# The end of an attention stage in an order written out by hand, with its output weights loaded in four pieces

## What is computed

```
x = x + _L0_xattn_ref(_layernorm(x), ctx_1024, cos, sin, ..., Wq, Wkv, Wo, bo)
    # lat, ctx = layer_norm(...); q = lat @ Wq; k, v = split(ctx @ Wkv)   16 heads of 64
    # k = apply_rope(k, cos, sin)
    # attn = clip(q k^T / 8, -11, 11); attn = softmax(attn); out = attn v
    # return out @ Wo + bo                     out: 4 x 128 x 1024, Wo: 1024 x 512
x = x + _L0_attn_ref(_layernorm(x), qkv_w, qkv_b, proj_w, proj_b)
x = x + _L0_ffn_ref(_layernorm(x), router_w, sg, su, sd, wg, wu, wd)
```

## Time and profile before

| | us |
|---|---|
| median of 3 runs | 1446.51 (1441.37 to 1452.56) |
| the profiled execution | 1454.4, its span 1452.7 |
| PE busy | 1394.5 (96%) |
| DVE, ACT, POOL busy | 850.0, 797.3, 833.6 |
| loop of `attend`, a step | about 8.1 |
| step 32 of the last batch to the start of `mix` | 1109.18 to 1164.85 |

### The profile page before, as it was taken

One profiled execution on the slowest core, in us unless ns is written; L12 is line 12 of the kernel. 1 busy time (PEld: TensorE's weight loads), 2 busy tenths in 40 slices (PEclk: granted clock), 3 DMA queues, 4 the chain that ended last, 5 costly groups with the idle time before them and its releaser, 6 DMA issues. The chain is left out here.

```text
span 1452.7 us, 25242 instructions
## 1 busy us (share of the span) xinstructions
PE 1394.5 (96%) x8758; PEld 1139.3 (78%) x8758; DVE 850.0 (59%) x1420; ACT 797.3 (55%) x1237; POOL 833.6 (57%) x723
## 2 busy tenths in 40 slices
PE   5899999999999999999999999999998889999998
PEld 3578888888788888878888888888887566766664
DVE  6456565666466566655565666656554356657564
ACT  3356566665566665656666656656555312346652
POOL 3267677776667776766777777777765324110002
PEclk9999999999999999999999999999999989899999
DMA  7567766766666676656677666776767380369994
GB/s 241 178 118 130 123 118 110 132 116 135 114 120 123 111 130 110 139 100 129 113 131 122 123 130 118 130 123 107 138 107 163 116 326 0 131 219 365 357 370 150
DMA packets 115219, 218.44 MB, mean 150 GB/s; under 512 B 13312, under 2 KB 49152, under 8 KB 108928
## 3 DMA queue, kind: packets, MB, share of 16 engines
q1 hardware_dynamic: 111920, 209.00, 63.8%
q0 software_dynamic: 1280, 4.20, 0.9%
q10 hardware_dynamic: 1872, 3.41, 0.6%
HBM read 132.67 MB, written 16.78 MB: 103 GB/s over the span
## 5 line engine op out<-in xcount | busy, mean ns | idle before, releaser
L605 POOL TENSOR_TENSOR p_parts<-probs,p_parts 128x512 fp32r<-128x512 f32 x256 | 340.3, 1349 | 252.2 <-ACT p_parts L660 252.2
L660 ACT ACTIVATE p_parts<-probs 128x512 fp32r<-128x512 f32 x256 | 147.7, 625 | 245.5 <-PE banks L914 237.9
L768 DVE TENSOR_TENSOR probs<-banks,probs 128x1024 f32<-128x1024 f32 x128 | 156.7, 1224 | 164.1 <-ACT probs L668 164.1
L709 ACT ACTIVATE probs<-probs 128x1024 f32<-128x1024 f32 x128 | 135.9, 1062 | 142.6 <-POOL probs L612 142.5
L866 PE MATMUL banks<-wv_hi,x_hi 128*128 128x512 f32 x512 | 208.5, 407 | 4.9 <-PEq L170 4.9
L867 PE MATMUL banks<-wv_lo,x_hi 128*128 128x512 f32 x512 | 202.8, 396 | 0.0
L881 PE MATMUL banks<-x_hi,wk_hi 128*128 128x512 f32 x512 | 201.8, 394 | 0.0
L868 PE MATMUL banks<-wv_hi,x_lo 128*128 128x512 f32 x512 | 201.8, 394 | 0.0
L883 PE MATMUL banks<-x_hi,wk_lo 128*128 128x512 f32 x512 | 199.6, 390 | 0.0
L882 PE MATMUL banks<-x_lo,wk_hi 128*128 128x512 f32 x512 | 199.3, 389 | 0.0
L910 PE MATMUL banks<-p_parts,v_hi 128*65 128x128 f32 x1024 | 192.0, 224 | 0.6 <-POOL p_parts L605 0.6
(11 more groups left out here) (291 smaller groups left out, 2694.5 us busy)
## 6 DMA issues: line engine op xcount, KB each, us to landing
queries<-q_scratch SPq DMA_DIRECT2D x256, 128.0 KB, 6.0
keys<-wo_room SPq DMA_DIRECT2D x128, 256.0 KB, 5.6
keys<-turned_odd SPq DMA_DIRECT2D x128, 256.0 KB, 5.6
row_room<-in_ctx SPq DMA_DIRECT2D x64, 256.0 KB, 6.2
wo_room<-in_down SPq DMA_DIRECT2D x10, 1024.0 KB, 7.1
wo<-in_gate SPq DMA_DIRECT2D x8, 1024.0 KB, 8.2
gate_raw<-in_up SPq DMA_DIRECT2D x8, 1024.0 KB, 10.2
up_raw<-in_gate SPq DMA_DIRECT2D x7, 1024.0 KB, 8.2
```

The lines of the kernel that those rows point to most:

```text
L605: nc.gpsimd.tensor_tensor(p_parts[:, 1, j, :], probs[:, pair % 2, j, :], p_parts[:, 0, j, :].bitcast(F32), ALU.subtract).then_inc(p_lo_rea ...
L768: nc.vector.tensor_tensor(mine, ps_s[:, :, :, 0, :].rearrange("p j i n -> p (j i) n"), mine, ALU.add).then_inc(s_taken, 1)
```

## The change

The steps that all engines share now end with step 31 of the last batch, and what follows is written out by hand for each engine.

- PE: in step 31 the value product is left out and put behind `weigh(26)`, in two halves around `score(28)`. From there on single output products, one, two or three at a time, stand between the scores and the weighings. A batch's sum now starts with tiles 4 to 7 (the second half of `wo`). All 8 products of batch 2 stand at the very end, behind the last `turn_sums`.
- ACT, DVE, POOL: the same instructions in another order. The low parts of the last two rotated keys move from POOL to DVE (`rope_low`). The four bias additions are parted in two pairs, the splits of the self attention's weights come later.
- `wo` is now two tensors of 4 tiles, `wo_first` and `wo_second`, in the first buffers of `x_hi` and `x_lo`, which are dead once chunk 2 of the last batch is done. SP loads it in four pieces of 512 KB in steps 25 to 28, for which it waits in step 24 for the key product of step 23. The loads of `x`, `bo` and of the three weights follow the last keys at once.
- The split weights of the self attention lie elsewhere (second buffers of `x_hi` and `x_lo`, `wk_hi`, `wk_lo`). The room of `wk_lo` (now `late_room`) is in use until the last qkv product, so in `mix` SP waits for `qkv_done` 12 where it waited for `wo_done`.

```
@@ SP
+                    wait(sp, k_ready, BATCH * BSTEPS - STEPS)
+                i = t - (BSTEPS - STEPS + 1)
+                if 0 <= i < KT:
+                    half, k = i // 2, i % 2 * 2
+                    sp.dma_start(wo[half][:, k:k + 2, :], d["wo"].rearrange("(t p) n -> p t n", p=P)[:, 2 * i:2 * i + 2, :]
+                                 ).then_inc(keep["wo_landed"], 16)
...
             run(sp, step)
+            wait(sp, s_ready, last_step - SCORE_LAG)
+            for pair in range(BSTEPS - 3, BSTEPS):
+                load_queries(LAST, pair)
+            store_keys(LAST, BSTEPS)
+
+            wait(sp, v_ready, last_step)
+            sp.dma_start(keep["x3"][:], d["x"].rearrange("b n d -> n b d")).then_inc(x_landed, 16)
...
@@ DVE
             run(dve, step)
+            rotate(LAST, 31)
+            finish(LAST, 25)
+            combine(LAST, BSTEPS, 0)
+            add_values(LAST, 26)
+            combine(LAST, BSTEPS, 1)
+            rope_low(0)
+            rope_low(1)
+            take_scores(LAST, 28)
+            values_low(LAST, 31)
+            finish(LAST, 26)
+            add_values(LAST, 27)
+            take_scores(LAST, 29)
+            finish(LAST, 27)
+            add_values(LAST, 28)
+            add_bias(0)
+            add_bias(1)
+            take_scores(LAST, 30)
...
@@ PE
+            for k in ks:
+                    if k == KT:
+                        wait(pe, keep["wo_landed"], 16 * KT)
+                        wait(pe, k_turned, last_step)
+                        wait(pe, keep["attn_t_ready"], max(2 * whose + 1, whose + 4 if whose else 0))
...
             run(pe, step)
+            values(LAST, 31, (0, 1))
+            score(LAST, 28)
+            values(LAST, 31, (2, 3))
+            turn_early(0)
+            turn_early(1)
+            turn_sums(LAST, 26)
+            weigh(LAST, 27)
+            score(LAST, 29)
+            turn_early(2)
+            turn_early(3)
+            project_early(0, (4, 5))
+            turn_sums(LAST, 27)
+            weigh(LAST, 28)
+            score(LAST, 30)
+            project_early(0, (6, 7))
+            turn_early(4)
+            project_early(0, (0,))
+            turn_sums(LAST, 28)
+            weigh(LAST, 29)
+            score(LAST, 31)
+            turn_early(5)
+            project_early(0, (1, 2, 3))
+            turn_sums(LAST, 29)
+            project_early(1, (4, 5))
+            weigh(LAST, 30)
+            project_early(1, (6, 7))
+            turn_sums(LAST, 30)
+            project_early(1, (0, 1))
+            weigh(LAST, 31)
+            project_early(1, (2, 3))
+            turn_sums(LAST, 31)
+            project_early(2, (4, 5, 6, 7, 0, 1, 2, 3))
...
@@ mix, SP
-            sp.wait_ge(wo_done, BATCH)
+            sp.wait_ge(qkv_done, 3 * BATCH)
```

More of the change, by code:

```diff
@@ L486, in run @@
                     step(b, t)
-            for t in range(STEPS, BSTEPS + VALUE_LAG + 2):
-                step(BATCH - 1, t)
+            for t in range(STEPS, BSTEPS):
+                step(LAST, t)
         def exists(b, t):
@@ L497, in ends_batch @@
             return exists(b, pair) and pair // STEPS % CHUNKS == CHUNKS - 1
-        def ends(b, t, n):
-            return isinstance(b, int) and b == BATCH - 1 and t == BSTEPS + n
         def row_tile_of(b, t):
@@ L633, in _ @@
             run(pool, step)
+            for pair in range(BSTEPS - VALUE_LAG, BSTEPS):
+                low_probs(LAST, pair)
+                clip(LAST, pair + 1)
         @block.scalar
@@ L696, in step, with exponents @@
+            def exponents(b, pair):
+                if exists(b, pair):
+                    wait(act, clipped, b * BSTEPS + (pair + 1))
+                    nc.scalar.activation(probs[:, pair % 2], probs[:, pair % 2], ACT.Exp, scale=SCALE).then_inc(probs_ready, 1)
+            def step(b, t):
+                high_probs(b, t - VALUE_LAG)
+                copy_scores(b, t - SCORE_LAG)
+                values_high(b, t - 1)
+                rope_high(b, t, 0)
                 tile = row_tile_of(b, t)
@@ L704, in step @@
                     out.then_inc(rows["full_ready"], 1)
[L706 to L712 removed]
+                exponents(b, t - SCORE_LAG)
+                rope_high(b, t, 1)
                 tile = row_tile_of(b, t - 1)
@@ L801, in split_low, with rope_low, add_bias @@
                                         ALU.subtract).then_inc(keep["qkv_lo_ready"], 1)
+            def rope_low(n):
+                group = BATCH * GROUPS - 1
+                slot = group % 2
+                part = parts_of(slot)[n]
+                wait(dve, rope_hi, 2 * group + (n + 1))
+                wait(dve, rope_lo, 2 * group + n)
+                nc.vector.tensor_tensor(part.bitcast(F32R), part, highs_of(slot)[n].bitcast(F32), ALU.subtract).then_inc(rope_lo, 1)
+            def add_bias(i):
+                if i == 0:
+                    wait(dve, x_landed, 32)
+                nc.vector.tensor_tensor(keep["x3"][:, i, :], keep["x3"][:, i, :], bo[:], ALU.add).then_inc(keep["x_ready"], 1)
             def step(b, t):
+                last = isinstance(b, int) and BSTEPS * b + t == last_step - 1
                 rotate(b, t - 1)
                 add_values(b, t - VALUE_LAG - 1)
-                if ends(b, t, 4):
-                    split_low(1)
                 combine(b, t, 0)
@@ L812, in step @@
                 take_scores(b, t - SCORE_LAG)
-                if ends(b, t, 3):
-                    split_low(0)
                 combine(b, t, 1)
                 values_low(b, t - 1)
-                finish(b, t - VALUE_LAG - 1)
+                if not last:
+                    finish(b, t - VALUE_LAG - 1)
                 tile = row_tile_of(b, t + 2) if t >= 1 else None
@@ L823, in step @@
                     row_tile_variance(nc, rows, dve, whole, tile % ROW_TILES)
-                if ends(b, t, 1):
-                    wait(dve, x_landed, 32)
-                    for i in range(BATCH):
-                        nc.vector.tensor_tensor(keep["x3"][:, i, :], keep["x3"][:, i, :], bo[:], ALU.add).then_inc(keep["x_ready"], 1)
                 if t % BSTEPS == STEPS - 1 and t > STEPS:
@@ L1828, in program @@
         keep = {"ident": sb("ident", [P, P]), "minus_half": sb("minus_half", [P, 8])}
-        keep["x_hi"] = sb("x_hi", [P, 2, KT, CHUNK], F32R)
+        with nc.sbuf_tensor("x_hi", [P, 2, KT, CHUNK], F32R) as keep["x_hi"]:
+            pass
+        keep["wo"] = [sb("wo_first", [P, 2, KT, DIM])[:, 0]]
         room = sb("row_room", [P, BATCH - 1, INNER])
```

174 lines of the change are left out of this document (89 added, 85 removed).

## The result

| | before | changed |
|---|---|---|
| median of 7 runs | 1446.76 us (1441.37 to 1452.56) | 1435.82 us (1432.80 to 1439.64) |
| ratio to before | | 0.9921, 95% interval 0.9895 to 0.9947 |
| the profiled execution | 1454.4, span 1452.7 | 1435.8, span 1434.1 |
| first score of step 31 to the start of `mix` | 63.79 | 48.89 |
| start of `mix` to the first qkv product | 14.57 | 11.02 |

The change gains 10.9 us, 0.8%. The two profiled executions lie 18.6 us apart, and the whole of it, 14.90 + 3.55 = 18.45 us, is in the two stretches that the change touches.

The account below looks back on a forecast made before the run. PE bounds the kernel, losing tail time to idleness and half clock. Tail -16.3, dip +1.2, `bo` and keys +0.6, `mix` start -3.3 gave -17.8 us; -17.5 from the 1446.5 median gave 1429 us, range 1422 to 1439.

Parts of the forecast that it names:

- PE's work: Tail from the point matching 1109.18: scores, transposes, sums with weighings and products at full clock, together 36.0 us.
- `bo`: Tail: bias lands at 1122.1, additions precede `take_scores(30)`, slack nearly nothing; 0.6 us taken for this and late keys.
- The first hole: Tail, second transpose group: PE waits 2.2 us for DVE's low part of step 31's value tile to free PSUM.
- The later holes: Tail: PE waits 0.5 us at `turn_sums(28)` for the scores of pair 30, then 0.2 us at the next.
- a dip behind the first hole: Tail: half clock after the 2.2 us wait at the second transpose group costs 0 to 1.5 us; 1.2 taken.
- The rival in which the whole tail runs at half clock: From the second transpose group PE's 35 us of work take twice as long; 1449 us, chance 0.03.
- The start of `mix`: First transposes to first qkv product: PE keeps full clock, DVE limits; 11.2 us for 14.6, so -3.3 us.
- The block's end: End of the tail: 0.35 us from the last instruction to the next block, as before.
- The pieces of `wo`: Steps 25 to 28: early loads behind key stores cost nothing; uncovered, each 1 MB pair up to 4.6 us.
- The zeros: `mix`: 4.3 MB start about 35 us later, issued at 1213, landing at 1232 before POOL scatters; cost nothing.
- The two late weight loads: `mix`: 2 MB of weights start after the last qkv product, about 35 us later; costed at nothing.
- the side that I had given 0.41: Whole kernel: chance 0.41 that the time changes by no more than 1%, between 1432.0 and 1461 us.

Follow-up runs that it names:

- Block of 8: Changed kernel with all eight output products of batch 0 in one block behind the weighing of pair 28; tail 54.42 us, median 1440.1 us.
- products inside: Changed kernel with all products of batch 2 and the last two of batch 1 ahead of the last weighing; tail 52.44, mix start 13.67, median 1440.9 us.
- output weights late: Changed kernel with the four `wo` pieces issued late, right ahead of the last queries, where the kernel before loads them; tail 54.70 us, median 1439.3 us.
- bias late: Changed kernel with the bias additions moved behind the next taking of scores, those of pairs 30 and 31; tail 46.77 us, medians 1434.9 and 1434.2 us.
- zeros first: Changed kernel with the two writes of zeros in `mix` ahead of the wait for the last qkv product; tail 48.89 us, median 1435.0 us.
- both holes: Changed kernel with later bias additions, plus one batch 0 output product moved between the first two transpose groups; tail 46.77 us, median 1434.4 us.
- Before, filled: Kernel before with 24 unused transposes of the identity behind PE's last sums; tail 60.06, mix start 11.04, median 1447.6 us, ratio 0.9992.
- the first comparison: Changed kernel against the kernel before, 7 runs of each; medians 1435.82 and 1446.76 us, ratio 0.9921.

## Why the prediction was right, and where its steps were off

**The mechanism.** The change gains by what was said: in the tail an alternation of chain and products gives way to products between the chain's steps. "Block of 8" undoes that alone and costs 5.5 us; "products inside" undoes the end alone and costs 6.2; "output weights late" undoes the loads alone and costs 5.8. Together that is 17.5 for a change of 16.4. Each part was undone by itself in the finished change, so that they nearly add up is no proof that they are independent. The moved value product of step 31 and the new order on ACT, DVE and POOL were not undone by any run.

**PE's work and the holes.** From the first score of step 31 the steps gave 1.0 + 7.1 (to 1109.18) + 36.0 + 3.0 + 0.35 = 47.5 us, with the clock and `bo` 49.3. Measured: 48.89, three times. The waits above 0.3 us are 1.77 + 1.96 + 0.34 = 4.1 of it and the rest 44.8, 0.7 more than reckoned. The first hole, 2.2 us and at the second transpose group, came at that place with 1.77. The forecast row of PE's idleness, near 3 us with one wait above 1 us, came out at 4.2 with two. The later holes, 0.5 and 0.2, did not come: without the wait for `bo` nothing was left of them ("bias late").

**`bo`.** "I take 0.6 for this and for keys" was too small. The slack was rightly seen as nothing, and the two additions ahead of `take_scores` were seen too. What was mis-sized is when `bo` lands: reckoned at 1122.1, which is 1120.55 from the change's own tail, it came at 1121.9 (issued at 1111.14, 10.8 us). Half a microsecond of that is the later issue of `x`, 0.65 the issue of `x` itself, which stands ahead of `bo` in SP's queue, and 0.2 the transfer. The score copy in turn ended at 1121.44, 0.4 us earlier than reckoned, so the whole 1.79 us of the additions lie on the path. It cost 2.1. The row that would have shown it wrong is the one I had named: no wait of DVE for `bo` beyond the score copy of pair 30.

**The clock.** The 1.2 us for a dip behind the first hole were too much: no trace of the change, nor of "zeros first", "bias late" or "both holes", has the tail below 1.00. That the sum of the tail came within 0.4 us is in part luck: `bo` and PE's work were 1.4 and 0.7 too small, the dip, the first hole and the later holes 1.2, 0.4 and 0.8 too large. The Trainium skill (TensorE: Matmul & The Clock Gate, section HAM oscillation) describes a kernel that falls back to half clock at every wait for data, with waits of about 3 to 5 us. The tail of before, with waits of up to 3.26 us, falls back in three traces; that of the change, with two waits under 2 us, does not, so the prediction stretched that rule when it said that by it the tail would not get the full clock at all. The rival in which the whole tail runs at half clock had no support, and its price was wrong: 35 us of work that take twice as long from 1110.7 on end at about 1180.7 and not at 1165.5. By its own terms it is about 16 us later than before, and no gain is left once about half of the work (not 0.9 of the tail) is at half clock.

**The start of `mix`.** -3.3 forecast, -3.55 measured, at full clock and with DVE next in line (the wait of 0.57 for `x_norm`). "Before, filled" gives 11.04 without the change, so the step is shown, not only argued. The block's end cost 0.34 for 0.35.

**What was costed at nothing.** The pieces of `wo` in steps 25 to 28 caused no wait of PE. Their old place would have cost 5.8 us, which the sum didn't need to know, since it was made from the new order; but it means that the new order needs the early loads, which the prediction didn't say. The zeros: nothing, shown. The two late weight loads: no wait seen, not tested by a run.

**The sum and the median.** -17.8 us were reckoned for the profiled execution, and the pair of traces gave -18.6. The step that was furthest off is the last: "part of that may be dips of just this kind, so I take -17.5 from the median". Of the 7.9 us by which that execution lay above the median I took off 0.3. Its tail and mix start were 2.1 us longer than the mean over three traces. With that taken off it is -15.7. The forecast of 1429 was 6.8 us too low, inside its range. Of this, 1.1 us is the change of the two stretches, 16.4 and not 17.5; 3.1 is the base, since the three executions of before had a median of 1446.5 and all 64 have a mean of 1449.6; 0.8 is the first comparison's median against the change's mean of 1435.0; and 1.8 stays open, little more than the 1.4 to which the difference of the means is known. The interval of the first comparison reaches from 8 to 15 us; a gain of 0.8% lies on the side that I had given 0.41, all executions together give 1.0%, right at the bound.

## What to carry to other kernels

When two kinds of work alternate on an engine, lay the chain of the one beside the prices of the other, piece by piece; a block of products ahead of the chain's next step costs the chain its length, and the idle time that it leaves pulls the clock down as well. Let the engine with the most work be the last to end a stage: here the ten products that stand behind the last weighing were worth 6.2 us, 2.65 of them in the next stage. And before a sum from one trace is set against a median, look at how the very stretch varies between traces: where the clock dips in it, one trace can be several microseconds off.

## What the runs showed of the hardware that I had not expected

- A loss of clock is not bound to the length of one wait. A wait of 2.03 and then one of 2.38 us in "block of 8" were followed by 0.50; a wait of 1.50 us at the end of `mix` was followed by half clock in both traces shown; but 1.77 and 1.96 us in the tail of the change, 14 us apart with dense work between, were in none of its three traces. The same wait can go either way: 2.18 us was followed by half clock in two traces of before and not in the third.
- The same kernel's half clock moves from trace to trace: in the tail of before its mean was 0.88, 0.90 and 0.93, and this goes with 3.5 us of time.
- Transfers of 2 MB ahead in the same queue lengthened the way of small transfers by 5.2 us (128 KB queries, 6.0 to 11.2) and 5.3 us (256 KB keys, 7.6 to 12.9). In the kernel before, where the keys are issued later behind the same 2 MB, it was 9.3 and 8.0.
